# A tower of layers on one core: in the last expert stage half of the tokens go through experts in order of expert

## Chip, core and metric

The kernel runs on one core of a Trainium2 chip. The metric is the device time of one execution in microseconds (us). Before the change it is 6574.02 us, the median of three runs.

## What is computed

The kernel is a stack of embedding, attention and feed-forward layers over 64 x 256 = 16384 tokens of 64 numbers. The change touches only the last feed-forward layer, in which each token goes through the best two of 16 experts:

```python
def _L3_ffn_ref(x, gate_w, gate_b, w1, w2, w3):
    logits = jnp.einsum('bsd,de->bse', x, gate_w) + gate_b
    probs = jax.nn.softmax(logits, axis=-1)
    top_probs, top_idx = jax.lax.top_k(probs, 2)
    top_probs = top_probs / jnp.sum(top_probs, axis=-1, keepdims=True)
    dispatch = jnp.sum(jax.nn.one_hot(top_idx, n_experts, dtype=x.dtype) * top_probs[..., None], axis=-2)
    h1 = jnp.einsum('bsd,edh->bseh', x, w1)
    h2 = jnp.einsum('bsd,edh->bseh', x, w2)
    hidden = jax.nn.silu(h1) * h2
    expert_out = jnp.einsum('bseh,eho->bseo', hidden, w3)
    return jnp.einsum('bseo,bse->bso', expert_out, dispatch)
...
h = h + _L3_ffn_ref(_layernorm(h, axis=-1), ...)
```

## The kernel before

All tokens live in SBUF as 128 tiles of 128 tokens: `H` is the residual stream, `X` a second array of that shape, `XT` the normed tokens turned, two tiles at a time (partitions 0 to 63 hold the numbers of one token, 64 to 127 those of a token of the other tile). Each part of the program is a `Stage`: it takes tiles and semaphores, runs one block of programs for the engines, and ends in a barrier of all engines. So an engine that is late holds the next stage. Inside a stage the order on each engine is the order in the code, and engines meet at semaphores.

The end of the program is four stages. `ln_f3` norms `H` and turns it into `XT`. `routd` (`route`) computes the 16 logits of each token (PE), the softmax and the two best experts (some 30 steps on DVE over 128x2048 numbers, each waiting for the one ahead of it, `link`), and turns the gates into `GT`; meanwhile SP loads the experts' matrices (`tables_d`). `expd` (`experts`) is dense: every token goes through every expert. It is a loop of 256 units, 16 blocks of 1024 tokens by 16 experts. One unit u is

- `hp` and `h`: x times w1 and x times w2 of the expert (L927, four products of 64 rows by 512 columns, the two halves of the array side by side),
- `gp`: the gate spread over 128 rows (L945, bf16),
- ACT: silu of `hp` (L1005); DVE: times `h` (L1041, the product), then times `gp` (L1046, the hidden part),
- `yp`: the hidden part times w3 (L959), added up in PSUM over the 16 experts.

On PE the order is gate(u), out(u-1), first(u+1), second(u+1). `h` and `gp` have one buffer each: second(u+1) waits until DVE has made product u, gate(u+1) until it has made hidden part u. After 16 units the block is turned back (L968) and DVE adds it to `H` (L1028). `store` writes `H` out.

Stages of other layers stand in for operations that `expd` lacks. `expb` gathers, for each of 64 samples, a row of weights per partition by an indirect transfer of POOL into six buffers `chosen` (L2190), multiplies 64x128 weights with 128 columns (L2217, 4 products), then the second matrices (L2230, 4 products), and turns back (L2238). `attd` is attention with f32 products of 128 columns or fewer. L2877 scatters 128 times 128 rows to DRAM, L3440 gathers as many.

## Time and profile before

| what | value |
|---|---|
| median of three runs (6570.31 to 6598.52) | 6574.02 us |
| the profiled execution's own time | 6573.63 us |
| its span | 6570.7 us |
| PE busy, share of the span | 81% |
| DVE, ACT, POOL busy | 78%, 40%, 31% |

The span is what the engines' instructions cover in the profiled execution; 2.9 us lie around it. Shares are means over many stages with different limits, and say nothing of the last stage alone.

### The profile page before, as it was taken

Reading aid. Unit: us, or ns where it says so; the run is one execution under the profiler, and the core shown is the slowest. Engines: PE = TensorE matmul, PEld = TensorE weight load, DVE = VectorE, ACT = ScalarE, POOL = GpSimd, SP = SyncE. Lnnn points to the kernel's source line nnn. Section 1 sums busy time; section 2 is a strip of 40 time slices with the busy share of each in tenths; the row PEclk is TensorE's granted clock in tenths of the full one; section 3 lists DMA queues with packets and bytes.
Section 4 is the critical chain, followed back from the end, with each engine's and each line's share of the span. In section 5 each row is a group of like instructions: output and inputs, shape, how many; then the busy total and the mean of one; then the engine's idle time right before and its main releaser. Section 6 shows DMA issues by size and latency. Waiting matters only on the chain. (4 is left out here: it accounts for less than half of the span.)

```text
span 6570.7 us, 109019 instructions
## 1 busy us (share of the span) xinstructions
PE 5313.6 (81%) x41259; PEld 3459.5 (53%) x41259; DVE 5093.1 (78%) x8887; ACT 2625.4 (40%) x4350; POOL 2046.0 (31%) x1992
## 2 busy tenths in 40 slices
PE   5668968885379999970899999999902899499998
PEld 3552246653246666650788888888801278333332
DVE  7878988886878888850798999989934677677776
ACT  3444433333256666640344444444411422233332
POOL 0010010003267600007777777777743010100000
PEclk8779989996689999975999999999956999699999
DMA  0200000112221000000222222222100000100001
GB/s 17 78 6 1 20 23 29 35 41 73 63 39 18 15 2 2 2 35 13 37 46 41 43 43 41 46 41 45 37 18 4 2 3 3 17 1 1 1 1 26
DMA packets 186692, 165.50 MB, mean 25 GB/s; under 512 B 87754, under 2 KB 167795, under 8 KB 184499
## 3 DMA queue, kind: packets, MB, share of 16 engines
q1 hardware_dynamic: 128814, 126.99, 6.6%
q0 software_dynamic: 57472, 32.64, 4.3%
q8 instruction: 274, 4.49, 0.3%
q14 instruction: 120, 0.98, 0.1%
q10 hardware_dynamic: 12, 0.39, 0.0%
HBM read 87.17 MB, written 50.67 MB: 21 GB/s over the span
## 5 line engine op out<-in xcount | busy, mean ns | idle before, releaser
L3043 PE MATMUL edges_bank<-part_room,hot_room 128*128 128x512 f32 x7168 | 1632.5, 390 | 190.4 <-DVE hot_room L3134 189.4
L3043 PEld LDWEIGHTS edges_bank<-part_room,hot_room 128*128 128x128 f32 x7168 | 1344.4, 188 | 478.6 <-issue 189.8
L3031 POOL DMA_INDIRECT XT<-gat_node_table,edges_idx x1152 | 1206.6, 1047 | 416.2 <-issue 413.2
L3064 ACT COPY XT<-edges_bank 128x512 f32<-128x512 f32 x896 | 524.5, 599 | 946.2 <-PE edges_bank L3043 943.3
L3152 DVE COPY_PREDICATED XT<-edges_tabs_p,XT 128x1024 f32<-128x1024 int32 (+3 forms) x896 | 634.2, 708 | 41.0 <-DVE edges_acc_s L3200 7.3
L3134 DVE TENSOR_SCALAR hot_room<-edges_lanes,edges_nodes 128x512 fp32r<-128x512 f16 x896 | 396.7, 503 | 102.1 <-PE edges_bank L3043 99.1
L1005 ACT ACTIVATE expd_act_out<-expd_hp 128x1024 f32<-128x1024 f32 x256 | 261.9, 1023 | 526.0 <-PE expd_hp L927 526.0
L1041 DVE TENSOR_TENSOR expd_act_out<-expd_act_out,expd_h 128x1024 f32<-128x1024 f32 x256 | 312.6, 1221 | 185.8 <-ACT expd_act_out L1005 185.8
L1460 ACT ACTIVATE GT<-attc_sc,attc_nm 128x256 f32<-128x256 f32 x1024 | 399.6, 480 | 37.0 <-DVE attc_nm L1526 36.9
L1474 ACT ACTIVATE GT<-attc_sct 128x1024 f32<-128x1024 f32 x256 | 262.2, 1024 | 325.0 <-PE attc_sct L1394 324.9
L1525 DVE TENSOR_REDUCE attc_mx<-attc_sc 128x4 f32<-128x1024 f32 x256 | 313.3, 1224 | 86.4 <-PE attc_sc L1383 86.2
L1383 PE MATMUL attc_sc<-XT,attc_tT 64*128 64x256 f32 x2048 | 295.2, 407 | 45.6 <-ACT GT L1460 45.5
L1046 DVE TENSOR_TENSOR expd_hid<-expd_act_out,expd_gp 128x1024 f32<-128x1024 f32 x256 | 312.5, 1221 | 8.8
L1530 DVE TENSOR_REDUCE attc_rs<-GT 128x4 f32<-128x1024 f32 x256 | 310.2, 1212 | 1.2 <-ACT GT L1460 1.2
L505 POOL TENSOR_TENSOR ln_f_xn<-H,ln_f_mean 128x1024 f32<-128x1024 f32 x4 | 11.4, 2846 | 945.5 <-DVE ln_f_shift L542 945.5
L927 PE MATMUL expd_hp<-XT,expd_in_w 64*128 64x512 f32 x1024 | 290.6, 644 | 2.4 <-PEq L82 2.1
L1404 PE MATMUL attc_op<-GT,attc_xB 128*64 128x256 f32 x2048 | 277.5, 391 | 6.8 <-ACT GT L1481 1.9
L959 PE MATMUL expd_yp<-expd_hid,expd_in_w 128*64 128x512 f32 x1024 | 276.2, 618 | 1.6 <-DVE expd_hid L1046 1.6
L1394 PE MATMUL attc_sct<-attc_tT,XT 64*128 64x256 f32 x2048 | 266.4, 377 | 1.6 <-DMA attc_tT<-attc_rT 1.0
L927 PE MATMUL expd_h<-XT,expd_in_wg 64*128 64x512 f32 x1024 | 263.3, 591 | 0.0
L1383 PEld LDWEIGHTS attc_sc<-XT,attc_tT 64*128 64x128 f32 x2048 | 185.1, 190 | 144.5 <-issue 116.5
L1766 ACT ACTIVATE X<-attb_r 128x2048 f32<-128x2048 f32 x64 | 120.1, 1877 | 267.8 <-PE attb_r L1723 267.8
(767 smaller groups left out, 9406.8 us busy)
## 6 DMA issues: line engine op xcount, KB each, us to landing
edges_lanes<-gat_places SPq DMA_DIRECT2D x224, 128.0 KB, 3.1
gat_states<-GT SPq DMA_DIRECT2D x32, 768.0 KB, 4.6
XT<-gat_node_table,edges_idx POOLq DMA_INDIRECT x1152
expert_pairs<-in_L_ffn_W_dram SPq DMA_DIRECT2D x48, 256.0 KB
XT<-XT SPq DMA_DIRECT2D x32, 256.0 KB
XT<-XT SPq DMA_DIRECT2D x64, 128.0 KB
XT<-XT SPq DMA_DIRECT2D x128, 64.0 KB
gat_starts<-nodes_zeros SPq DMA_DIRECT2D x4, 1088.0 KB, 8.0
```

The source lines that it names most:

```text
L927: m = nc.tensor.matmul(bank[:, odd, :], w[half, e, :], g.XT[half, i * U:(i + 1) * U], start=True, stop=True)
L1041: nc.vector.tensor_tensor(act_out[:, u % 2], act_out[:, u % 2], h2[:], ALU.mult).then_inc(product_ready, 1)
L1046: nc.vector.tensor_tensor(hid[:, u % 2], act_out[:, u % 2], gp[:], ALU.mult).then_inc(hid_full, 1)
L1383: m = nc.tensor.matmul(sc[(0, 1, 1, 0)[hp]][:, n, a * S:(a + 1) * S], tT[half, b % NB, hp, a * P:(a + 1) * P], x(b, half), start=True, sto ...
L1460: m = nc.scalar.activation(prob[:, hp % 2, n, a, :], sc[(0, 1, 1, 0)[hp]][:, n, a * S:(a + 1) * S], ACT.Exp, bias=nm[:, b % 2, n, hp, a:a ...
L1525: link(vec.tensor_reduce(best, sc[(0, 1, 1, 0)[hp]][:].rearrange("p n (a s) -> p n a s", s=S), AX.X, ALU.max))
L1530: vec.reduce_sum(rs[:, b % 2, :, hp, :], prob[:, hp % 2], AX.X).then_inc(totaled, 1)
L3031: nc.gpsimd.indirect_dma_start(out=rows[:, k, c, :], out_offset=None, in_=q.t_table, in_offset=bass.IndirectOffsetOnAxis(ap=idx[:, k, c:c ...
L3043: m = nc.tensor.matmul(banks[t % BANKS][:], hot[:, (k * GROUPS + j) % 2, b, t, :], parts[:, p, b].rearrange("p u c -> p (u c)"), start=b = ...
L3064: nc.scalar.copy(fetched[:, (k * GROUPS + j) % 2, t].rearrange("p u c -> p (u c)"), banks[t % BANKS][:]).then_inc(fetched_in, 1)
L3134: m = vec.tensor_scalar(hot[:, (k * GROUPS + j) % 2, b], lanes[:, j], nodes[:, b:b + 1], None, ALU.is_equal)
L3152: vec.copy_predicated(half(0, w), taken(s, w), half(w, 2 * w)).then_inc(halved, 1)
```

## The change

The last layer is cut in two. Token tiles 0 to 63 stay dense, as two calls of `experts` with 4 blocks (64 units) each, `expd` and `expe`. Tiles 64 to 127 are sorted by expert. Each of their tokens has two slots in a DRAM array `sorted_in`, where an expert's slots begin at a multiple of 256; 2 x 8192 slots and at most 15 partly filled tiles make `COUNT` = 79 tiles of 256 slots, whatever the data.

- `ln_f3` keeps the normed tokens in `X` too. `route_sorted` takes the place of `route`: gates for the dense half alone, and for the sorted half the slot of each (token, choice), by two bf16 products with a triangle and with ones, a scan over tiles and experts, and a sum; and the row of weights for each tile and partition. SP clears `sorted_in` (5.2 MB of zeros) and lays out `expert_rows`, 1280 bytes for each expert and partition, behind the loads that it had.
- `expd`: POOL scatters, meanwhile, 64 tiles x 2 choices = 128 indirect transfers of 128 rows of 256 bytes.
- `exps` (`sorted_experts`) is new: 79 tiles. SP loads a tile (64 KB, six buffers), POOL gathers the weights of its expert (160 KB, six buffers), PE turns the tile by a plain product with the identity, multiplies (4 products of 64x128 weights with 128 columns), multiplies with w3 (2 products), turns back by a plain product; DVE and ACT move data between, and SP stores 64 KB to `sorted_out`. It starts when all scatters have landed.
- `expe`: POOL fetches, meanwhile, both rows of each sorted token by 128 indirect transfers; DVE takes them eight token tiles at a time (`collect.add`), after every eighth unit: times the gates, sum of two, plus `H`. The last such group comes behind the last unit.

The core of the diff:

```diff
+    def __init__(self, nc, g, st, W1, W2, W3):
+        self.nc, self.g = nc, g
+        self.sources = W1, W2, W3
+        self.E = E = W1.shape[0]
+        self.COUNT = 2 * SORTED * P // SLOTS_TILE + E - 1
+        self.slot = st.sb("slot", [P, SORTED, 2], I32)
...
+        n = self.COUNT * SLOTS_TILE // P
+        sp.dma_start(self.rows_in.rearrange("(p n) d -> p n d", p=P), bc(self.zeros, 1, n)).then_inc(self.cleared, 16)
+        for half in (slice(0, D), slice(D, P)):
+            sp.dma_start(rows[:, half, 0:P], W1).then_inc(self.built, 16)
+            sp.dma_start(rows[:, half, P:2 * P], W2).then_inc(self.built, 16)
+        sp.dma_start(rows[:, :, 2 * P:], W3).then_inc(self.built, 16)
...
+    def scatter(self, pool):
+        pool.wait_ge(self.cleared, 16)
+        for t in range(SORTED):
+            for c in range(2):
+                self.nc.gpsimd.indirect_dma_start(
+                    out=self.rows_in, out_offset=bass.IndirectOffsetOnAxis(ap=self.slot[:, t, c:c + 1], axis=0),
+                    in_=self.g.X[:, TILES - SORTED + t, :], in_offset=None).then_inc(self.scattered, 16)
+
+    def fetch(self, pool):
+        back = self.g.X[:].rearrange("p (t c) d -> p t c d", c=2)
+        for t in range(SORTED):
+            for c in range(2):
+                self.nc.gpsimd.indirect_dma_start(
+                    out=back[:, t, c, :], out_offset=None, in_=self.rows_out,
+                    in_offset=bass.IndirectOffsetOnAxis(ap=self.slot[:, t, c:c + 1], axis=0)).then_inc(self.fetched[t // 8], 16)
+
+    def add(self, v, link, k, target):
+        vec, t = self.nc.vector, slice(8 * k, 8 * k + 8)
+        y = self.g.X[:].rearrange("p (t c) d -> p t c d", c=2)[:, t]
+        x = target[:, TILES - SORTED + 8 * k:TILES - SORTED + 8 * k + 8, :]
+        v.wait_ge(self.fetched[k], 256)
+        link(vec.tensor_tensor(y, y, bc(self.gate[:, t, :], 3, D), ALU.mult))
+        link(vec.tensor_tensor(y[:, :, 0, :], y[:, :, 0, :], y[:, :, 1, :], ALU.add))
+        link(vec.tensor_tensor(x, x, y[:, :, 0, :], ALU.add))
...
+                link(vec.tensor_tensor(sort.gate[:], sort.gate[:], bc(total[:, DENSE:], 2, 2), ALU.mult))
...
+                link(vec.tensor_copy(tot, pl[:, 1].rearrange("p t e -> p e t")))
+                flat = [a.rearrange("p e t -> p (e t)") for a in (first, keep, tot)]
+                link(vec.tensor_tensor_scan(flat[0], flat[1], flat[2], 0.0, ALU.mult, ALU.add))
...
+                link(vec.tensor_tensor(rank, first.rearrange("p e t -> p t e"), pl[:, 0], ALU.add))
+                link(vec.tensor_tensor(prod, hots, bc(rank, 1, 2), ALU.mult))
+                link(vec.reduce_sum(place, prod, AX.X))
+                link(vec.tensor_copy(sort.slot[:].rearrange("p t c -> p c t"), place))
+                link(vec.tensor_tensor(reach, bc(number[:], 2, E), bc(end[:], 1, COUNT), ALU.is_ge))
+                link(vec.reduce_sum(expert[:], reach, AX.X))
+                link(vec.tensor_scalar(expert[:], expert[:], float(E - 1), float(P), ALU.min, ALU.mult))
+                link(vec.tensor_scalar(sort.weight_row[:], expert[:], g.lane[:], None, ALU.add))
...
+def sorted_experts(nc, g, name, sort):
+
+    COUNT = sort.COUNT
+    NX, NW, NY, NH = 6, 6, 4, 3
+    LAG = NX + 5
...
+                sp.wait_ge(sort.scattered, 16 * 2 * SORTED)
+                for i in range(COUNT + LAG):
+                    if i < COUNT:
+                        if i >= NX:
+                            sp.wait_ge(x_turned, i - NX + 1)
+                        sp.dma_start(xs[:, i % NX], rows_in[i]).then_inc(loaded[i % NX], 16)
+                    k = i - LAG
+                    if k >= 0:
+                        sp.wait_ge(rows_ready, k + 1)
+                        sp.dma_start(rows_out[k], ys[:, k % NY]).then_inc(stored[k % NY], 16)
...
+                for j in range(COUNT):
+                    if j >= NW:
+                        pool.wait_ge(used, j - NW + 1)
+                    nc.gpsimd.indirect_dma_start(
+                        out=chosen[:, j % NW, :], out_offset=None, in_=sort.weights,
+                        in_offset=bass.IndirectOffsetOnAxis(ap=sort.weight_row[:, j:j + 1], axis=0)).then_inc(gathered[j % NW], 16)
...
+                def turn(j):
+                    pe.wait_ge(loaded[j % NX], 16 * (j // NX + 1))
+                    if j:
+                        pe.wait_ge(x_moved, j)
+                    nc.tensor.matmul(pt[:, 0:P], xs[:, j % NX].rearrange("p a d -> p (a d)"), g.ident[:], start=True, stop=True).then_inc(x_turned, 1)
+
+                def hidden(j):
+                    pe.wait_ge(gathered[j % NW], 16 * (j // NW + 1))
+                    pe.wait_ge(x_moved, j + 1)
+                    if j >= 2:
+                        pe.wait_ge(hid_full, j - 1)
+                    for n in range(2):
+                        for a, half in enumerate(halves):
+                            m = nc.tensor.matmul(hp[j % 2][:, a, n * P:(n + 1) * P], chosen[half, j % NW, n * P:(n + 1) * P],
+                                                 xT[half, j % 2, :], start=True, stop=True)
+                    m.then_inc(hp_full, 1)
+
+                def out(j):
+                    pe.wait_ge(hid_full, j + 1)
+                    if j >= 2:
+                        pe.wait_ge(y_moved, j - 1)
+                    for a, half in enumerate(halves):
+                        m = nc.tensor.matmul(yp[j % 2][half, 0:P], chosen[:, j % NW, 2 * P:], hid[:, j % NH, a, :],
+                                             start=True, stop=True)
+                    m.then_inc(used, 1)
+
+                def turn_back(j):
+                    pe.wait_ge(y_moved, j + 1)
+                    if j:
+                        pe.wait_ge(rows_ready, j)
+                    nc.tensor.matmul(yt[:, 0:P], yT[:, j % 2, :], g.ident[:], start=True, stop=True).then_inc(y_turned, 1)
+
+                turn(0)
+                for i in range(COUNT + 3):
+                    if i + 1 < COUNT:
+                        turn(i + 1)
+                    if i < COUNT:
+                        hidden(i)
+                    if 2 <= i < COUNT + 2:
+                        out(i - 2)
+                    if i >= 3:
+                        turn_back(i - 3)
...
+                        nc.scalar.activation(act_out[:, i % 2], hp[i % 2][:, :, 0:P], ACT.Silu).then_inc(act_done, 1)
...
+                def move_x(j):
+                    v.wait_ge(x_turned, j + 1)
+                    if j >= 2:
+                        v.wait_ge(hp_full, j - 1)
+                    vec.tensor_copy(xT[:, j % 2, :], pt[:, 0:P]).then_inc(x_moved, 1)
+
+                def move_rows(j):
+                    v.wait_ge(y_turned, j + 1)
+                    if j >= NY:
+                        v.wait_ge(stored[j % NY], 16 * (j // NY))
+                    vec.tensor_copy(ys[:, j % NY].rearrange("p a d -> p (a d)"), yt[:, 0:P]).then_inc(rows_ready, 1)
+
+                move_x(0)
+                for i in range(COUNT + 4):
+                    if i + 1 < COUNT:
+                        move_x(i + 1)
+                    if i >= 4:
+                        move_rows(i - 4)
+                    if i < COUNT:
+                        v.wait_ge(act_done, i + 1)
+                        if i >= NH:
+                            v.wait_ge(used, i - NH + 1)
+                        vec.tensor_tensor(hid[:, i % NH], act_out[:, i % 2], hp[i % 2][:, :, P:2 * P], ALU.mult).then_inc(hid_full, 1)
...
+def experts(nc, g, name, tables, target=None, hide=0, measure=False, first_block=0, blocks=None, spread=None, collect=None):
 
     E, F, gated = tables.E, tables.F, tables.gated
...
+                    if collect is not None and u and u % COLLECT == 0:
+                        collect.add(v, link, u // COLLECT - 1, target)
...
+                if collect is not None:
+                    for k in range((NU - 1) // COLLECT, SORTED // 8):
+                        collect.add(v, link, k, target)
...
-    turned_norm(nc, g, "ln_f3", g.H, known=True)
+    turned_norm(nc, g, "ln_f3", g.H, keep=g.X, known=True)
     with Stage(nc, "expd_in") as kept:
         tables_d = ExpertTables(nc, kept, I["L3_ffn_w1"], I["L3_ffn_w3"], Wg=I["L3_ffn_w2"])
-        route(nc, g, "routd", I["L3_ffn_gate_w"], I["L3_ffn_gate_b"], 16, probs=True, ahead=tables_d)
-        experts(nc, g, "expd", tables_d, target=g.H)
+        sort = ExpertSort(nc, g, kept, I["L3_ffn_w1"], I["L3_ffn_w2"], I["L3_ffn_w3"])
+        route_sorted(nc, g, "routd", I["L3_ffn_gate_w"], I["L3_ffn_gate_b"], sort, ahead=tables_d)
+        experts(nc, g, "expd", tables_d, target=g.H, blocks=4, spread=sort)
+        sorted_experts(nc, g, "exps", sort)
+        experts(nc, g, "expe", tables_d, target=g.H, first_block=4, blocks=4, collect=sort)
```

What the order on the engines becomes. First PE, where `expd` now ends and the sorted stage begins (`exps_pt` is the turned tile, `exps_hp` the two first products, `exps_yp` the output, `exps_yt` the tile turned back). Before, these rows stood there, with no end:

```order
L927 MATMUL expd_hp<-XT,expd_in_w 128x512 x2
L927 MATMUL expd_h<-XT,expd_in_wg 128x512 x2
L945 MATMUL expd_gp<-GT,expd_in_pick 128x512 x2
L959 MATMUL expd_yp<-expd_hid,expd_in_w 64x512 x2
L927 MATMUL expd_hp<-XT,expd_in_w 128x512 x2
```

And now, after 64 such units:

```order
L1271 MATMUL expd_yp<-expd_hid,expd_in_w 64x512 x4
L1280 MATMUL expd_yt<-ident,expd_yT 128x128 x4
L1216 UNCONDITIONAL_BRANCH
L1098 UNCONDITIONAL_BRANCH
L1104 MATMUL exps_pt<-ident,XT 128x128 x2
L1113 MATMUL exps_hp<-exps_xT,exps_chosen 128x128 x4
L1104 MATMUL exps_pt<-ident,XT 128x128
L1113 MATMUL exps_hp<-exps_xT,exps_chosen 128x128 x4
L1104 MATMUL exps_pt<-ident,XT 128x128
L1113 MATMUL exps_hp<-exps_xT,exps_chosen 128x128 x4
L1122 MATMUL exps_yp<-exps_hid,exps_chosen 64x128 x2
L1130 MATMUL exps_yt<-ident,exps_yT 128x128
```

Per tile PE has eight products of 128 columns, in the order turn of the next tile, first products of this one, output of the one two ahead, turn back of the one three ahead.

POOL had nothing behind the routing stage:

```order
L832 IOTA routd_rev 128x16
L779 MEMSET GT 128x4096
L872 MEMSET expd_in_pick 128x1024
L879 AFFINE_SELECT expd_in_pick<-expd_in_pick 128x2048 x6
L707 UNCONDITIONAL_BRANCH
```

Now it issues 335 indirect transfers, one group in each of the three stages:

```order
L878 DMA sorted_in<-X,expd_in_slot 20224x64 x128
L1216 UNCONDITIONAL_BRANCH
L81 ISA
L1088 UNCONDITIONAL_BRANCH
L1094 DMA exps_chosen<-expert_rows,expd_in_weight_row 128x320 x79
L1072 UNCONDITIONAL_BRANCH
L81 ISA
L1222 UNCONDITIONAL_BRANCH
L886 DMA X<-sorted_out,expd_in_slot 128x64 x128
```

A stage's barrier now waits for POOL to have issued its group.

On DVE the two steps of a unit alternated without a break but for L1028:

```order
L1041 TENSOR_TENSOR expd_act_out<-expd_act_out,expd_h 128x1024
L1046 TENSOR_TENSOR expd_hid<-expd_act_out,expd_gp 128x1024
L1041 TENSOR_TENSOR expd_act_out<-expd_act_out,expd_h 128x1024
L1046 TENSOR_TENSOR expd_hid<-expd_act_out,expd_gp 128x1024
L1041 TENSOR_TENSOR expd_act_out<-expd_act_out,expd_h 128x1024
```

In `expe` three steps of `collect.add` stand between two units, seven times, and once at the end:

```order
L1353 TENSOR_TENSOR expe_act_out<-expe_act_out,expe_h 128x1024
L1358 TENSOR_TENSOR expe_hid<-expe_act_out,expe_gp 128x1024
L895 TENSOR_TENSOR X<-X,expd_in_gate 128x1024
L896 TENSOR_TENSOR X<-X 128x8x64
L897 TENSOR_TENSOR H<-H,X 128x512
L1353 TENSOR_TENSOR expe_act_out<-expe_act_out,expe_h 128x1024
L1358 TENSOR_TENSOR expe_hid<-expe_act_out,expe_gp 128x1024
```

## Rows read from the trace of the kernel before

**Rows 1.** Windows; busy us (count) by engine, granted clock, DMA share, GB/s.

```profile
...
5735.00:5800.00 65.00, 65.00 (x294) 20.41 (x290) 50.14 (x42) 22.06 (x22) 0.00 (x0) 1.00 0.00 1
```

**Rows 2.** Timeline, one steady unit of `expd`; start, length, engine.

```profile
...
6100.85 1.22 DVE L1046 TENSOR_TENSOR expd_hid<-expd_act_out,expd_gp 128x1024 f32<-128x1024 f32 x1
...
6101.47 1.02 PE L927 MATMUL expd_h<-XT,expd_in_wg 64*128 64x512 f32 x4
...
6102.33 0.38 PE L945 MATMUL expd_gp<-GT,expd_in_pick 64*128 64x512 bf16 x2
...
6102.74 1.22 DVE L1041 TENSOR_TENSOR expd_act_out<-expd_act_out,expd_h 128x1024 f32<-128x1024 f32 x1 [0.67 <-ACT expd_act_out L1005]
```

**Rows 3.** Timeline: start and end of `expd`, and the final store.

```profile
...
5721.16 3.76 ACT L804 COPY GT<-routd_gt 128x1024 bf16<-128x1024 bf16 x4 [0.21 <-PE routd_gt L798]
...
5725.80 0.53 PEld L927 LDWEIGHTS expd_hp<-XT,expd_in_w 64*128 64x128 f32 x4 [2.21 <-issue]
...
5733.26 1.08 PE L959 MATMUL expd_yp<-expd_hid,expd_in_w 128*64 128x512 f32 x4
...
6541.85 1.08 PE L959 MATMUL expd_yp<-expd_hid,expd_in_w 128*64 128x512 f32 x4
...
6546.94 0.69 DVE L1028 TENSOR_TENSOR H<-H,expd_yt 128x512 f32<-128x512 f32 x1 [2.51 <-PE expd_yt L968]
6548.77 14.26 SPq L1089 DMA_DIRECT2D out_dram<-H  x4
```

**Rows 4.** Timeline: two whole-width steps at the end of routing on DVE.

```profile
...
5705.02 2.29 DVE L829 TENSOR_TENSOR routd_G<-routd_G,routd_total 128x2048 f32<-128x2048 f32 x1
...
5714.52 1.23 DVE L789 CAST GT<-X 128x2048 bf16<-128x2048 f32 x1
```

**Rows 5.** Groups of POOL: issuing indirect scatters of 128 rows each.

```profile
...
L2877 POOL DMA_INDIRECT gat_starts<-gat_a_dst,gat_start_row x128 | 124.1, 969 | 82.3 <-issue 41.4 <-DVE gat_a_dst L2860 40.9
```

**Rows 6.** Timeline: the per-sample stage `expb` at the high clock.

```profile
...
1691.34 0.72 PE L2217 MATMUL expb_hp<-XT,expb_chosen 64*128 64x128 f32 x8
...
1691.98 0.66 PE L2230 MATMUL expb_yp<-expb_hid,expb_chosen 128*64 128x128 f32 x8
...
1692.49 1.30 POOL L2190 DMA_INDIRECT expb_chosen<-expert_pairs,expb_idx  x1 [0.30 <-issue]
...
1692.57 0.33 PE L2238 MATMUL expb_yt<-ident,expb_yT 128*128 128x128 f32 x1
...
1692.83 0.71 PE L2217 MATMUL expb_hp<-XT,expb_chosen 64*128 64x128 f32 x8
```

**Rows 7.** Timeline: plain f32 products with 128x128 weights in `attd`.

```profile
...
5457.05 0.59 PE L1940 MATMUL attd_r<-attd_both,XT 128*128 128x192 f32 x2
...
5457.57 0.33 PE L1949 MATMUL attd_r<-attd_vz,attd_kd 128*32 128x32 f32 x16
...
5457.83 0.66 PE L1955 MATMUL attd_r<-attd_wp,attd_oT 128*128 128x64 f32 x4
...
5458.42 1.08 PE L1977 MATMUL attd_r<-X,attd_vz 128*32 128x128 f32 x32
```

**Rows 8.** Groups of DVE: the 128x128 copy out of PSUM.

```profile
...
L2068 DVE COPY attd_vz<-attd_r 128x128 f32<-128x128 f32 x37 | 10.4, 280 | 0.0
```

**Rows 9.** DMA issues: KB each, median us to landing.

```profile
...
edges_lanes<-gat_places SPq DMA_DIRECT2D x224, 128.0 KB, 3.1
```

**Rows 10.** Timeline: `expb` at a granted clock of 0.50.

```profile
...
1575.79 0.48 PE L2238 MATMUL expb_yt<-ident,expb_yT 128*128 128x128 f32 x1
...
1578.40 0.48 PE L2238 MATMUL expb_yt<-ident,expb_yT 128*128 128x128 f32 x1
```

**Rows 11.** Windows, columns as in rows 1: `expb` twice, then the start of `expd`.

```profile
...
1600.00:1650.00 50.00, 29.35 (x225) 20.62 (x225) 21.88 (x42) 15.17 (x40) 14.86 (x13) 0.60 0.55 144
1660.00:1700.00 40.00, 37.56 (x423) 26.69 (x422) 37.70 (x93) 27.25 (x75) 30.30 (x23) 1.00 0.42 119
5725.00:5733.00 8.00, 6.85 (x20) 2.40 (x20) 2.44 (x2) 3.14 (x3) 0.00 (x0) 0.58 0.00 1
```

More of the change, by code:

```diff
@@ L687, in top2_steps, with route @@
     return vector_part, pool_part, act_part
-def route(nc, g, name, Wr, br, E, ahead, probs=False):
+def route(nc, g, name, Wr, br, E, ahead):
     with Stage(nc, name) as st:
@@ L758, in _, with __init__ @@
             def _(act):
-                if probs:
-                    act.wait_ge(shifted, 1)
-                    nc.scalar.activation(L, L, ACT.Exp).then_inc(exped, 1)
-                else:
-                    parts["act"](act)
+                parts["act"](act)
                 gates.scalar(act)
+SORTED, SLOTS_TILE, COLLECT = TILES // 2, 2 * P, 8
 class GateSplit:
-    def __init__(self, nc, g, st, E, scratch):
-        self.nc, self.g, self.E = nc, g, E
-        self.g3 = g.GT[:, TOKENS // 2:].rearrange("p (t c) -> p t c", c=D)
-        self.rest = scratch
+    def __init__(self, nc, g, st, E, scratch, tiles=TILES):
+        self.nc, self.g, self.E, self.tiles = nc, g, E, tiles
+        self.g3 = g.GT[:, TOKENS // 2:].rearrange("p (t c) -> p t c", c=D)[:, 0:tiles]
+        self.rest = scratch[:, 0:tiles]
         self.pt = [st.ps(f"gt{k}", [P, 8 * P], BF16) for k in range(2)]
@@ L792, in tensor @@
         pe.wait_ge(self.split, 1)
-        for c in range(TILES // 16):
+        for c in range(self.tiles // 16):
             if c >= 2:
@@ L801, in scalar @@
     def scalar(self, act):
[L802 removed]
+        for c in range(self.tiles // 16):
             act.wait_ge(self.turned, c + 1)
             self.nc.scalar.copy(self.g.GT[:, c * 8 * P:(c + 1) * 8 * P], self.pt[c % 2][:]).then_inc(self.moved, 1)
[L807 to L835 removed]
 class ExpertTables:
@@ L882, in gpsimd, with sync, clear @@
                 pool.wait_ge(self.picked, done)
-def experts(nc, g, name, tables, target=None, hide=0, measure=False):
+class ExpertSort:
+    def __init__(self, nc, g, st, W1, W2, W3):
[4 more added lines that the diff above has]
+        self.slot = st.sb("slot", [P, SORTED, 2], I32)
+        self.gate = st.sb("gate", [P, SORTED, 2])
+        self.weight_row = st.sb("weight_row", [P, self.COUNT], I32)
+        self.zeros = g.stats[:].rearrange("p t s -> p (t s)")[:, 0:D]
+        self.rows_in = nc.dram_tensor("sorted_in", [self.COUNT * SLOTS_TILE, D], F32).ap()
+        self.rows_out = nc.dram_tensor("sorted_out", [self.COUNT * SLOTS_TILE, D], F32).ap()
+        self.weights = nc.dram_tensor("expert_rows", [E * P, 5 * D], F32).ap()
+        self.built, self.blank, self.cleared, self.scattered, self.own = (
+            st.sem(n) for n in ("rows_built", "blank", "rows_cleared", "scattered", "sort_own"))
+        self.fetched = [st.sem(f"fetched{k}") for k in range(SORTED // 8)]
+    def sync(self, sp):
+        W1, W2, W3 = self.sources
+        rows = self.weights.rearrange("(e p) f -> e p f", e=self.E)
+        sp.wait_ge(self.blank, 1)
+        n = self.COUNT * SLOTS_TILE // P
[4 more added lines that the diff above has]
+        sp.dma_start(rows[:, :, 2 * P:], W3).then_inc(self.built, 16)
+    def clear(self):
+        self.nc.gpsimd.memset(self.zeros, 0.0).then_inc(self.blank, 1)
+    def scatter(self, pool):
[20 more added lines that the diff above has]
+        link(vec.tensor_tensor(x, x, y[:, :, 0, :], ALU.add))
@@ L887, in experts @@
+def experts(nc, g, name, tables, target=None, hide=0, measure=False, first_block=0, blocks=None, spread=None, collect=None):
     E, F, gated = tables.E, tables.F, tables.gated
     U = 512
-    NB = TOKENS // (2 * U)
+    NB = TOKENS // (2 * U) if blocks is None else blocks
     NU = NB * E
@@ L915, in _ @@
                     g.order.sync(sp)
+            @block.gpsimd
+            def _(pool):
+                if spread is not None:
+                    spread.scatter(pool)
+                if collect is not None:
+                    collect.fetch(pool)
             @block.tensor
@@ L926, in hidden @@
                     for odd, half in enumerate(halves):
-                        m = nc.tensor.matmul(bank[:, odd, :], w[half, e, :], g.XT[half, i * U:(i + 1) * U], start=True, stop=True)
+                        m = nc.tensor.matmul(bank[:, odd, :], w[half, e, :], g.XT[half, (first_block + i) * U:(first_block + i + 1) * U], start=True, stop=True)
                     return m
@@ L944, in gate @@
                     for odd, half in enumerate(halves):
-                        m = nc.tensor.matmul(gp[:, odd, :], pick[half, e, :], g.GT[half, i * U:(i + 1) * U], start=True, stop=True)
+                        m = nc.tensor.matmul(gp[:, odd, :], pick[half, e, :], g.GT[half, (first_block + i) * U:(first_block + i + 1) * U], start=True, stop=True)
                     m.then_inc(gp_full, 1)
@@ L1053, in _ @@
                 add(NB - 1)
+                if collect is not None:
+                    for k in range((NU - 1) // COLLECT, SORTED // 8):
+                        collect.add(v, link, k, target)
                 if measure:
```

219 lines of the change are left out of this document (177 added, 42 removed).

## Prediction

> **What bounds the kernel now.** I read the page for the whole, then windows over the last stage, then its timeline. In `expd` PE is busy in 100 us of 100, at a granted clock of 1.00, with DVE at 78 and ACT at 33 [rows 1]. In the timeline DVE is what sits idle: it waits 0.67 us in each unit for ACT [rows 2], which by the code waits for `hp` of PE. So PE is the bound, and the stage costs PE's time per unit. The first `yp` of the stage starts at 5733.26 and the one of unit 254 at 6541.85, so a unit takes (6541.85 - 5733.26) / 254 = 3.183 us, turns back included. The stage runs from 5725.80 to 6546.94 + 0.69 = 6547.63: 821.8 us, of which 256 x 3.183 = 814.9, and 7.0 are filling and emptying [rows 3].
>
> **Removed, and what stays dense.** Two dense stages of 64 units take the place of one of 256: each 64 x 3.183 + 7.0 = 210.7, together 421.4 us.
>
> **The sorted stage, per tile.** PE has eight f32 products of 128 columns. Six of them stand in `expb`, with the same shapes and operands of the same kind. There the four first products take 1691.98 - 1691.34 = 0.64 us from start to start, at the high clock; the four second ones 1692.57 - 1691.98 = 0.59, so the two that are left here some 0.30 [rows 6]. A turn is a plain product with 128x128 weights, which no row has at 128 columns. `attd` brackets it: one of 192 columns takes 5457.57 - 5457.05 = 0.52 us, and two of 64 columns take 5458.42 - 5457.83 = 0.59, 0.295 each [rows 7]. The line between them gives 0.41 for 128 columns. The turn of `expb`, which is in transpose mode, takes 0.26 [rows 6]; that is the lower bound, 0.52 the upper. I take 0.41, twice. A tile: 0.41 + 0.64 + 0.30 + 0.41 = 1.76 us; with the bounds 1.46 to 1.98.
>
> What could be slower than PE? DVE has two copies of 128x128 at 0.28 [rows 8] and a product of 256 columns, below the 0.69 of 512 [rows 3]: at most 1.25 us. ACT has silu over 256 columns and a copy of 128, no more than DVE's work. POOL issues one gather per tile; undisturbed one takes 0.97 us [rows 5] and 0.30 between two [rows 6], 1.27 in all; beside DVE's adds in `expb` 1.30 + 0.30 = 1.60 [rows 6]. All lie below 1.76. The waits in a circle: a tile buffer of weights is reused six tiles on, and the gather may be issued once the output of tile j-6 is made, four tiles ahead of its use: 4 x 1.76 = 7.0 us for 1.27 of issue and the landing. A load of 128 KB lands in 3.1 us [rows 9], so this holds if landing stays under 5.7. Bytes: 160 KB of weights, 64 in and 64 out per tile, 295 KB in 1.76 us = 168 GB/s. `expb` moves 119 GB/s at a DMA share of 0.42 [rows 11], in proportion 0.59 here, and more for the shorter packets. It fits, not with much room.
>
> 79 tiles x 1.76 = 139.0. Before the first turn come a barrier and a load (3.1), behind the last tile three more steps of the pipeline and a store (3.1): about 10 together. The stage begins behind idle time, as `expd` did before, and I let it start at the low clock (1.2 GHz of 2.4) as well: in the first 8 us of `expd` the granted clock is 0.58 [rows 11]. A cycle of `expb` takes 2.61 us at the low clock (1578.40 - 1575.79) [rows 10] and 1.49 at the high one (1692.83 - 1691.34) [rows 6], a factor of 1.75; 8 us at the low clock lose 3.4. The sorted stage: 139.0 + 10 + 3.4 = 152 us.
>
> **The scatters in `expd`.** 128 scatters took (124.1 + 41.4) / 128 = 1.29 us each [rows 5]. So POOL is done after 165 us of the stage's 210.7 and lies wholly beside PE; it would show only above 1.65 us each. The 1.60 of `expb` [rows 6] makes 205, still covered. Rows here are 256 bytes, 16384 of them; the final store moves as many runs of 256 bytes from 6548.77 to the end of the span at 6570.7, in 22 us [rows 3], so bandwidth isn't the question. The zeros (20224 runs of 256 bytes, by the same rate 27 us) and the weights' rows stand on SP behind loads that were there, in a routing stage of 100 us; the scatters wait for the zeros alone. I cost them at nothing; uncovered they would cost at most 40.
>
> *A page on it:* the Trainium skill, "GPSIMD Engine Reference", section "Key points", says that GpSimd shares its SBUF interfaces with VectorE and contends with instructions that have two SBUF inputs. The trace agrees: POOL's issue took 1.30 us beside adds of two SBUF tiles against 0.97 undisturbed. The two steps of an `expd` unit read one SBUF tile and one in PSUM, so by the page the 1.29 holds there; without the page's distinction 1.60 would hold, and the sum is the same.
>
> **The fetches and adds in `expe`.** 16 gathers must land for each eight units: 16 x 1.29 = 20.7 us against 8 x 3.183 = 25.5. Covered. The adds are new work of DVE: 1024, 512 and 512 columns; at 0.69 for 512 [rows 3] that is 1.2 + 0.7 + 0.7 = 2.6 us in one piece. The next product waits anyway 0.67 us for ACT. Behind it PE has little slack: hidden part u ends at 6102.07 and the gate product that waits for it starts at 6102.33, 0.26 [rows 2]. So each piece stops PE for 2.6 - 0.67 - 0.26 = 1.7 us; seven of them, 12, and the eighth stands uncovered behind the last unit, 2.6: 14.5 us. Bounds: 2.6 alone if all is made up, 8 x 2.6 = 21 if nothing is.
>
> **Routing.** A step over 128x2048 takes 2.29 us [rows 4]. Four steps on gates and five of the split shrink to half: 4 x 1.15, and 2 x 1.15 + 3 x 0.62 of the split with its casts (1.23), -9 us. Added behind them are six steps of 1024 numbers, two of 2048, two of 1264, a scan of 1024 and a dozen small ones: 6 x 1.15 + 2 x 2.3 + 2 x 1.4 + 1.2 to 2.4 + 2 = 18 us. But the old stage went on for 9 us after DVE's last cast (5714.52 + 1.23) until the gates were copied (5724.92) [rows 3, 4], and DVE's new steps lie beside that. Net 0 to +1; I take +1, bounds -1 to +4.
>
> **Barriers.** From the last copy of `routd` (5721.16 + 3.76) to the first weights of `expd` (5725.80) pass 0.9 us [rows 3]; two more: 1.8.
>
> **Sum.** 421.4 + 152 + 14.5 + 1 + 1.8 = 590.7 against 821.8: -231.1. The profiled span becomes 6570.7 - 231.1 = 6339.6, with the 2.9 around it 6342.5. The profiled execution (6573.63) and the median (6574.02) differ by 0.4: predicted 6343. The bounds of the terms (1.46 to 1.98 a tile: -24 to +17; adds -12 to +6; routing -2 to +3) give 6305 to 6369.
>
> **Rivals.**
>
> *A, data for the tiles comes late.* Between 1600 and 1650 `expb` issued 13 gathers, 3.85 us a sample, with PE busy 59% and the DMA share at 0.55 [rows 11]: weights can be late, there beside other transfers of SP. For it: three streams at once, and only four tiles of lead. Against it: between 1660 and 1700 the same loop ran at its PE bound. A landing of 8 us makes (8 + 1.27) / 4 = 2.3 us a tile, 79 x 0.55 = +43: 6386. Chance 0.18.
>
> *B, the clock stays low in the sorted stage.* `expb` stayed at 0.50 with PE's products in close order [rows 10], and had 0.60 between 1600 and 1650 [rows 11]. Then a tile takes 1.76 x 1.75 = 3.08 us: 79 x 1.32 - 3.4 = +101: 6444. For it: short products with waits between. Against it: `expb` also kept 1.00 at 94% busy [rows 11]. The Trainium skill, "TensorE: Matmul & The Clock Gate", section "PE-mode transpose", says that transposes don't count as busy for the clock; the turns here are plain products, which would make B less likely, and no row here shows that by itself. Chance 0.12.
>
> *C, indirect transfers of 256-byte rows are slower to issue than the rows shown.* At 2.0 us each, 128 make 256 us, both dense stages grow by 45: 6433. For it: no row has 256 bytes. Against it: in `expb`, whose rows are 1536 bytes, the issue took 1.30 beside adds, and in the scatters, whose rows are 16 bytes, 0.97 [rows 5, 6]; a hundredfold length moved it less than the threshold of 1.65. The Trainium skill, "DMA: Bandwidth & Descriptors", section "Specifications", puts the shortest transfer at full rate at 512 bytes and calls shorter ones read-modify-write; by it the landing suffers, while the issue, which is the term here, does not. Chance 0.07.
>
> *D, slower than before.* A, far worse: the sorted stage eats the gain when a tile takes (139 + 231) / 79 = 4.68 us, which is a landing of 17 us. The worst stretch of `expb`, 3.85, gives 6343 + 79 x 2.09 = 6508; at 5.0 us a tile it would be 6599. Chance 0.03.
>
> That the change doesn't do what it says is hardly possible: 79 tiles and 128 units are fixed, whatever the data.
>
> **How the numbers follow.** The forecast has 0.60, with 6305 to 6369. A 0.18, B 0.12, C 0.07, D 0.03. The range 6300 to 6440 holds the forecast, A, C and milder forms of B, and leaves out most of B and D. A measurement of this kernel tells about 0.5% (33 us) from no change: faster 0.96, within it 0.01, slower 0.03.
>
> **What the profile after would show.** Two dense stages of some 211 and 225 us with PE at 100%; between them a stage of 152 with 79 gathers 1.76 us apart, PE near 100% and the clock 1.00 after its start; POOL done with its scatters 45 us ahead of the barrier; DVE pieces of 2.6 us each with a PE gap of 1.7. Wrong it would be by first products that wait for `exps_chosen` (A, D), a clock near 0.5 between the dense stages (B), or POOL as the last at a barrier or `collect.add` waiting for its rows (C).

## The result, and the profile after

The changed kernel takes 6337.5 us, the median of 4 runs (6328.9 to 6341.7); the kernel before, in 4 runs, 6572.2. The ratio is 0.9634, with a 95% interval of 0.9605 to 0.9663. The forecast was 6343, in a range of 6300 to 6440. The profiled execution took 6341.45 us with a span of 6339.7, 231.0 us under the span of before.

Windows of the changed kernel, with the columns of [rows 1]: `expd`, the start of the sorted stage `exps`, its steady part, and `expe`.

```profile
5736.00:5946.00 210.00, 206.62 (x912) 65.14 (x912) 158.50 (x132) 69.18 (x69) 122.74 (x128) 0.99 0.06 21
5949.00:5965.00 16.00, 15.53 (x83) 11.20 (x84) 4.62 (x15) 3.15 (x10) 7.56 (x8) 0.50 0.51 144
5971.00:6083.00 112.00, 112.00 (x1086) 84.03 (x1087) 61.47 (x204) 43.05 (x136) 62.83 (x67) 1.00 0.67 177
6093.00:6313.00 220.00, 208.06 (x912) 64.09 (x908) 175.70 (x152) 67.89 (x68) 122.81 (x128) 0.99 0.10 20
```

PE is the bound of all three stages; in `expe` it stands idle for 12 us of 220, which are the adds below. In the steady part of `exps` it is busy in 112 us of 112 at a clock of 1.00. The second line is the surprise: 16 us at 0.50 (1.2 GHz), with PE busy in 15.5 of them.

The timeline of PE in the steady part shows what a tile costs:

```profile
6042.67 0.44 PE L1122 MATMUL exps_yp<-exps_hid,exps_chosen 128*64 128x128 f32 x4
6043.04 0.49 PE L1130 MATMUL exps_yt<-ident,exps_yT 128*128 128x128 f32 x2
6043.36 0.39 PE L1104 MATMUL exps_pt<-ident,XT 128*128 128x128 f32 x2
6043.68 0.71 PE L1113 MATMUL exps_hp<-exps_xT,exps_chosen 64*128 64x128 f32 x8
6044.32 0.44 PE L1122 MATMUL exps_yp<-exps_hid,exps_chosen 128*64 128x128 f32 x4
```

From start to start: outputs 0.37, the turns 0.32 each, first products 0.64; the tile 6044.32 - 6042.67 = 1.65 us.

The boundary between routing and `expd`, from the timeline of the changed kernel, where the old one had [rows 3, 4]:

```profile
5714.68 0.69 DVE L776 CAST GT<-XT 128x1024 bf16<-128x1024 f32 x1
...
5718.21 2.29 DVE L1007 TENSOR_TENSOR_SCAN XT<-XT 128x1024 f32<-128x1024 f32 x1
...
5718.64 1.93 ACT L791 COPY GT<-routd_gt 128x1024 bf16<-128x1024 bf16 x2 [0.21 <-PE routd_gt L785]
...
5734.60 0.26 DVE L1025 TENSOR_SCALAR expd_in_weight_row<-routd_expert,lane 128x79 int32<-128x79 f32 x1
5736.02 2.08 PE L1239 MATMUL expd_hp<-XT,expd_in_w 64*128 64x512 f32 x4 [16.50 <-PEq L82]
```

The gates are copied at 5720.57, and DVE goes on alone for 14 us; PE waits 16.5 us at the barrier.

An add piece in `expe`, from the timeline of the changed kernel:

```profile
6123.30 1.22 DVE L895 TENSOR_TENSOR X<-X,expd_in_gate 128x1024 f32<-128x1024 f32 x1
...
6124.55 0.69 DVE L896 TENSOR_TENSOR X<-X 128x512 f32<-128x512 f32 x1
6124.96 1.13 PE L1239 MATMUL expe_hp<-XT,expd_in_w 64*128 64x512 f32 x4
6125.28 0.69 DVE L897 TENSOR_TENSOR H<-H,X 128x512 f32<-128x512 f32 x1
...
6127.28 1.13 PE L1239 MATMUL expe_h<-XT,expd_in_wg 64*128 64x512 f32 x4 [1.19 <-DVE expe_act_out L1353]
...
6129.86 1.13 PE L1239 MATMUL expe_hp<-XT,expd_in_w 64*128 64x512 f32 x4
```

`hp` to `hp` takes 4.90 us here, 3.15 in an undisturbed unit: the piece costs 1.75 us.

The groups of POOL; the last columns are busy time, mean, and idle time:

```profile
L886 POOL DMA_INDIRECT X<-sorted_out,expd_in_slot x128 | 123.0, 961 | 50.7 <-issue 38.7 <-SPq L1216 12.0
L878 POOL DMA_INDIRECT sorted_in<-X,expd_in_slot x128 | 122.7, 959 | 128.7 <-SPq L1216 87.3 <-issue 41.4
```

(122.7 + 41.4) / 128 = 1.28 us for a scatter.

**The span, term by term.** The first normalising step of `ln_f` on DVE (the reciprocal) started at 5600.42 before and starts at 5605.78 now: 5.4 us of drift in stages that nothing touches. From there to `expd`'s first weights it was 125.4 us and is 130.2: +4.8 for routing. Then, from the first weights of `expd` to the last add of `expe`, 580.5 us (`expd` 210.3, `exps` with its barriers 146.1, `expe` 224.1) against 821.8: -241.3. What comes behind is 0.1 longer. The sum is 5.4 + 4.8 - 241.3 + 0.1 = -231.0.

### The profile page after: what moved, and what is told of

It is laid out like the page before. It is cut to its first block and busy times, and to the rows that moved or that the text cites. A ratio compares the mean times of both kernels' runs of the same rounds, so it can differ in the third digit from the quotient of the medians.

```text
span 6339.7 us, 108731 instructions
## 1 busy us (share of the span) xinstructions
PE 5054.9 (80%) x40671; PEld 3433.3 (54%) x40671; DVE 4882.0 (77%) x8912; ACT 2538.3 (40%) x4368; POOL 2373.4 (37%) x2332
## 5 line engine op out<-in xcount | busy, mean ns | idle before, releaser
L1711 PEld LDWEIGHTS attc_sct<-attc_tT,XT 64*128 64x128 f32 x2048 | 204.7, 188 | 21.1 <-DMA attc_tT<-attc_rT 1.9
L2379 DVE TENSOR_TENSOR X<-attd_r,attd_decay 128x2048 f32<-128x2048 f32 x64 | 146.7, 2291 | 82.2 <-PE attd_r L2282 82.1
L1721 PEld LDWEIGHTS attc_op<-GT,attc_xB 128*64 128x64 f32 x2048 | 129.4, 136 | 128.0 <-issue 94.0
L2127 DVE TENSOR_REDUCE attb_mx<-attb_r 128x16 f32<-128x2048 f32 x64 | 146.4, 2287 | 65.7 <-PE attb_r L2026 65.6
```

What stands on the lines that cost most here:

```text
L1711: m = nc.tensor.matmul(sct[:, n, j * S:(j + 1) * S], x(b, half)[:, j * P:(j + 1) * P], tT[half, b % NB, hp, :], start=True, stop=True)
L1721: m = nc.tensor.matmul(op[half, 0:S], xB[:, b % NB, j, (2 * hp + n) * D:(2 * hp + n + 1) * D], probT[:, hp % 2, n, j, :], start=hp + j == ...
```

## The experiments

A run's whole time drifts: the same kernel reached routing's first product at 5635.1, 5641.9 and 5626.2 us in three executions. So I compare the lengths of four stretches: routing (first `logits` product to first `hp`), `expd` (to the end of its last add), `exps` (to the first `hp` of `expe`), `expe` (to the first store). The code of the edits is abridged.

```
kernel         chip  routing   expd    exps    expe
changed          -    101.0    210.2   146.1   225.8
e0_again         A    101.0    210.1   146.4   225.8
e1_transpose     A    101.0    210.1   161.3   225.7
e2_direct        A    100.9    210.1   222.8   226.6
e3_spread        A    101.0    210.1   146.4   213.0
e4_later         B     92.5    366.3   144.7   377.3
e5_warm          B    101.0    362.6   146.1   377.0
e6_lead          B    101.0    363.4   189.7   378.0
e7_twice         B    101.0    527.2   146.9   376.8
e9_best          C     92.5    214.1   146.5   212.9
e10_wide         C    101.0    210.3   132.0   225.9
e11_twice        C    101.0    210.1   264.2   226.6
e12_again        C    101.0    210.1   148.8   225.7
```

Three chips were used, each in one batch of runs. On A the kernel before took 6573.5 us, on C 6569.3, on B 7877.9. Of the runs in the table only the changed kernel and e9 were executed more than once, four times each.

**e0_again.** 

> The changed kernel once more, unaltered, to see how far the lengths of single stages repeat: expd 210.3, exps 146.1, expe 224.2 us, each within 0.5 us; the stages ahead may differ by some us in sum.

The stages repeat within 0.3 us. Over all runs that leave the sorted loop alone `exps` repeats less well: 144.7 us (e4) to 148.8 (e12), without e5. What differs is how long the granted clock stays at 0.50 behind the first turn: 14 us in e4, 17 in the changed kernel, 23 in e12. So a difference of some 2 us in `exps` says nothing.

**e1_transpose.**

```
-  nc.tensor.matmul(pt[:, 0:P], xs[...], g.ident[:], start=True, stop=True)
+  nc.tensor.transpose(pt[:, 0:P], xs[...], g.ident[:])
   (the turn back likewise)
```

> Both turns of the sorted stage in PE's transpose mode in place of plain products with the identity; nothing else. In the profile after, the two turns together take 0.64 us and a tile 1.655 us. (a) A turn costs what the one of expb costs, 0.26 us: a tile 1.53 us, the stage 9 us shorter than its 146.1. (b) Both forms cost the same: stage unchanged, 146. (c) Turns in transpose mode keep the clock low for longer than the first 16.5 us: each tile at the low clock costs 1.3 us more; low throughout it would be 214 us and more. I expect (a).

Measured: 161.3 us, 15 longer. Windows of e1_transpose over `exps`:

```profile
5950.00:6000.00 50.00, 50.00 (x295) 31.50 (x293) 18.89 (x63) 13.65 (x42) 19.80 (x22) 0.50 0.47 126
6000.00:6020.00 20.00, 20.00 (x190) 13.43 (x190) 11.15 (x41) 8.29 (x26) 12.43 (x14) 0.91 0.66 181
6020.00:6040.00 20.00, 17.70 (x180) 11.58 (x177) 10.76 (x40) 8.26 (x26) 12.69 (x14) 1.00 0.73 203
6040.00:6080.00 40.00, 40.00 (x248) 25.45 (x248) 15.37 (x51) 11.04 (x34) 15.82 (x17) 0.53 0.48 128
```

It is (c), with (a) inside it: where the clock is 1.00 a tile is shorter than with plain products, but the clock is 0.50 for the first 58 us and falls again later. PE in the timeline of e1_transpose at the clock of 1.00:

```profile
6028.53 0.33 PE L1130 MATMUL exps_yt<-ident,exps_yT 128*128 128x128 f32 x1
6028.70 0.27 PE L1104 MATMUL exps_pt<-ident,XT 128*128 128x128 f32 x1
6028.90 0.71 PE L1113 MATMUL exps_hp<-exps_xT,exps_chosen 64*128 64x128 f32 x8
6029.54 0.44 PE L1122 MATMUL exps_yp<-exps_hid,exps_chosen 128*64 128x128 f32 x4
6029.91 0.33 PE L1130 MATMUL exps_yt<-ident,exps_yT 128*128 128x128 f32 x1
```

The two turns take 6028.90 - 6028.53 = 0.37 us in place of 0.64, and a tile 6029.91 - 6028.53 = 1.38 us, where (a) had 1.53. At 0.50 a tile takes 2.40. By the Trainium skill, "TensorE: Matmul & The Clock Gate", section "PE-mode transpose", transposes don't count as busy for the clock; this trace agrees, with PE busy in 50 us of 50 at 0.50. It does not single the transposes out, since the next run has such a stretch without any.

**e2_direct and e10_wide.** In both the second products come out as rows, with no turn back:

```
-  matmul(yp[half, 0:P], chosen[:, 2*P:], hid[:, a, :])      # then ACT copy, turn_back, DVE copy
+  matmul(yp[:, a*D:(a+1)*D], hid[:, a, :], chosen[:, 2*P:])   # e2: 64 columns, ACT copies to ys
+  matmul(yp[:, a*P:(a+1)*P], hid[:, a, :], chosen[:, 3*D:])   # e10: 128 columns, half not used
```

> The second products of the sorted stage with the hidden values as weights and the expert's matrix as 64 columns, so that rows come out with slots on partitions: the turn back, ACT's copy for it and DVE's second copy are gone. (a) Such a product costs what those of 64 columns in attd cost, 0.295 us: 0.59 for the two in place of 0.37 + 0.32, a tile 1.56 us, and one step of the pipeline less behind the last tile: the stage 9 us shorter than 146.1. (b) With only 64 columns to hide it, the load of 128x128 weights sets the pace and the product costs 0.4 us: a tile 1.77, the stage 8 us longer. (c) PE is not what bounds the stage: no change. I expect (a).

> As e2_direct (hidden values as weights), but with 128 columns moved in each second product instead of 64; the additional 64 columns (a part of another matrix) are made and not used. In e2_direct the granted clock was 0.50 in the whole sorted stage, 2.73 us a tile with PE busy all the time. (a) It was the 64-column products that kept the clock low: with 128 columns it comes back to 1.00, a tile takes 0.32 + 0.64 + 0.64 = 1.60 us, the stage about 143 us. (b) It was the exchange of weights and moved operand, or the missing turn: the clock stays at 0.50, a tile takes over 2.8 us, the stage 225 us or more. I expect (a).

Measured: e2 222.8 us, e10 132.0. Windows of e2_direct, then of e10_wide:

```profile
5965.00:6020.00 55.00, 55.00 (x283) 45.95 (x282) 14.64 (x41) 13.10 (x40) 18.89 (x20) 0.50 0.41 109
6020.00:6170.00 150.00, 150.00 (x771) 125.39 (x770) 39.12 (x110) 35.67 (x110) 51.02 (x54) 0.50 0.39 107
```

```profile
5974.00:6050.00 76.00, 75.86 (x708) 63.73 (x706) 35.83 (x101) 32.40 (x100) 47.53 (x51) 1.00 0.70 197
```

And PE in the timeline of e10_wide:

```profile
6030.30 0.71 PE L1121 MATMUL exps_yp<-exps_chosen,exps_hid 128*128 128x128 f32 x4
6030.84 0.39 PE L1103 MATMUL exps_pt<-ident,XT 128*128 128x128 f32 x2
6031.16 0.72 PE L1112 MATMUL exps_hp<-exps_xT,exps_chosen 64*128 64x128 f32 x8
6031.81 0.71 PE L1121 MATMUL exps_yp<-exps_chosen,exps_hid 128*128 128x128 f32 x4
```

None of e2's three cases foresaw it. PE was busy in 205 us of 205 (5965 to 6170), as my case (a) has it, but at 0.50 to the end of the stage, where its tile of 2.73 us makes the stage 77 us longer. e10 has the same order of products and moves 128 columns in the second ones: the clock is 1.00 from 12 us behind the last add of `expd` on, the two products take 0.54 us, a tile 1.51 (1.60 expected), and the stage is 14 us shorter than that of the changed kernel, 17 shorter than e12's on the same chip. So the exchange of weights and moved operand, (b), is not what kept e2 at 0.50, since e10 has it too; case (a) of e10 holds. Nor is it the share of weight loads: PEld is busy in 84% of the stretch in both (125.39 of 150, 63.73 of 76). e2 ran on chip A and e10 on chip C; the unaltered kernel came to a clock of 1.00 on both, so the chip is an unlikely cause.

**e3_spread.**

```
-  if u and u % COLLECT == 0: collect.add(v, link, u // COLLECT - 1, target)
+  if u >= 7 and u % 7 < 3 and u // 7 <= SORTED // 8:
+      collect.add(v, link, u // 7 - 1, target, u % 7)      # one of the three steps
-  for k in range((NU - 1) // COLLECT, SORTED // 8): collect.add(...)   # behind the last unit
```

> The adds of expe in 24 single steps instead of 8 pieces of three: one step behind the DVE work of each of units 7, 8, 9, then 14, 15, 16 and so on, the last at 58, none behind the last unit. (a) A step stalls PE only by what exceeds 0.93 us (DVE's wait for ACT and PE's slack): 0.3 for the gate step of 1.22 us, nothing for the two of 0.69: expe falls from 224.2 us to 210.7 + 2.4 = 213. (b) Every step of DVE stalls PE by its whole length: 8 x 2.6 = 21 us, expe 231. (c) The stall comes from waiting for the fetched rows, not from DVE's time: expe longer than 224, with DVE waiting for DMA. I expect (a).

Measured: `expe` 213.0, 12.8 us shorter. (a) holds: the units behind which a gate step stands are 0.15 to 0.35 us longer, 2.4 in all, and no other step shows. The burst cost the time, not DVE's work.

**e9_best, with e4_later in it.** e4 issues the steps from L1019 on in `expd`:

```
+  if spread is not None and u < len(spread.later): step = spread.later[u](); link(step)
+  pool.wait_ge(self.placed, 1)            # in scatter(), before the first one
```

> DVE's last seven steps of routing (slots and weight rows, 5726.45 to 5734.86 in the profile after, 8.4 us) are issued in expd instead, one behind the DVE work of each of the first seven units; the scatters wait for the third. (a) The routing stage gets 8.4 us shorter, and expd loses only what exceeds 0.93 us in each step: 1.4 + 1.4 + 0.6 + 0.6 = 4.0 us; net -4.4 from the end of the norm to the start of the sorted stage. (b) DVE's time comes back whole: net 0. (c) The scatters start some 12 us later and become the last at the barrier: not by the rows, they were done 46 us ahead. I expect (a).

> The adds of expe in single steps (as in e3_spread, which took 12.8 us from expe) together with the deferred routing steps (as in e4_later, which took 8.4 us from routing). Expected on a chip where scatters do not disturb PE: routing 92.5, expd 210.3 + 4.0 = 214.3, exps 146.1, expe 212.9: 17 us under the changed kernel, 0.3%, and about 0.961 of the kernel before. If DVE's deferred time comes back whole, expd is 218.7 and the gain is that of the adds alone, 13 us.

e4 ran on chip B, where `expd` can't be compared (below); its routing is 8.5 us shorter. e9, on chip C, has the same 92.5 and an `expd` of 214.1, +4.0 against e12 on the same chip, where 4.0 was expected. e9 took 6315.8 us (4 runs), 0.9611 of the kernel before (0.9595 to 0.9627), and 19.4 us less than e12_again on the same chip; 2.3 of these lie in `exps`, where e12 was late to the high clock, so the two edits are worth the 17 us forecast. The interval overlaps with that of the changed kernel's ratio; it is the stages that show the gain. e10's edit lies in another stage. By an estimate from e10's `exps`, 132.0 in place of 146.5, both together would come to some 6301; that was not run.

**e12_again.** 

> The changed kernel unaltered, as the measure for the other three: routing 100.9, expd 210.3, exps 146.1, expe 225.7 us to the store. On a chip where the scatters hold up PE: expd near 363, expe near 377, and then more time than the kernel before.

`exps` is 2.4 us longer than in e0: two more tiles ran at a granted clock of 0.50, at 2.93 us in place of 1.66. The others repeat.

**e5_warm.**

```
+  for _ in range(3): nc.tensor.matmul(pt[:], g.ident[:], g.XT[:, 0:512], start=True, stop=True)
   turn(0)
```

> Three f32 products of 512 columns whose result is not used stand ahead of the first turn of the sorted stage, in the 3.4 us in which PE waits for the first load. (a) The low clock of the stage's first 16.5 us (granted 0.50) comes from that idle stretch: filled, the low stretch is short or gone, and the stage some 7 us shorter than 146.1. (b) The clock has fallen for the barrier's idle time already, or the short products of the fill do not bring it back: the low stretch stays at some 16 us and the stage within 1 us. The granted clock between the barrier and the tenth tile tells. I expect (a), with little confidence.

Measured: 146.1, no change that shows beside the 144.7 and 146.9 of e4 and e7 on the same chip. (b) is right on the stage's length; on the clock neither case is right. Windows of e5_warm from the start of the stage:

```profile
7394.00:7398.00 4.00, 2.50 (x4) 1.26 (x5) 0.69 (x1) 0.00 (x0) 1.56 (x2) 0.76 0.22 57
7398.00:7402.00 4.00, 3.52 (x17) 1.86 (x15) 0.58 (x2) 0.14 (x1) 3.08 (x4) 0.82 0.66 192
7402.00:7406.00 4.00, 2.45 (x25) 1.71 (x25) 1.58 (x5) 1.06 (x4) 1.66 (x3) 1.00 0.54 155
7406.00:7410.00 4.00, 4.00 (x24) 3.10 (x26) 1.28 (x5) 0.65 (x2) 1.33 (x2) 0.54 0.21 65
7410.00:7414.00 4.00, 4.00 (x29) 2.89 (x26) 1.13 (x4) 1.28 (x4) 0.98 (x2) 0.61 0.49 129
```

The granted clock fell to 0.50 at 7396.1, 2.1 us behind the last dense product and in the first of the three, rose to 1.00 at 7399.5, and was 0.50 again from 7406.3 to 7413.1, behind a stretch in which PE, in the filling pipeline, was busy 2.45 us of 4. It is back at 1.00 for good 18.4 us behind the last add, 19.4 in the changed kernel. The fillers also held the first turn back: 5.1 us behind the last add instead of 2.7. That the one gain and the other loss cancel is argued from these numbers, not tested.

**e6_lead.** `NW` is 4 in place of 6.

> Four buffers for gathered weights instead of six. A buffer is busy for wait and issue (1.25 us), landing (3.1), then from the first product to the output two tiles on, 2T + 1.0 us. (a) If the weights' way round the buffers bounds, 4T = 5.35 + 2T gives T = 2.7 us a tile, the stage 146 + 79 x 1.0 = 227 us; with six buffers the same sum gives 1.34, below PE's 1.655, which is why data was not late there. (b) If landing is short when the queue is less loaded, T stays near 1.66 and the stage at 146. I expect (a).

Measured: 189.7 us, (189.7 - 146.1) / 79 = 0.55 more a tile: 2.2 us, with 38.0 us of PE's waits for `exps_chosen`. (a) in kind, half its size; solved backwards, 4T = x + 2T + 1.0 gives x = 3.4 us for issue and landing, not 5.35 - 1.0 = 4.35. With six buffers weights would be late from x = 5.6 on.

**e7_twice and e11_twice.** The same edit, on chips B and C:

```
-  for c in range(2):
-      indirect_dma_start(out=self.rows_in, ...)
+  for c, rows in ((0, self.rows_in), (1, self.rows_in), (0, self.again), (1, self.again)):
+      indirect_dma_start(out=rows, ...)
```

> Each scatter of expd is issued twice, the second time into a scratch array that nobody reads: 256 instead of 128. (a) POOL's issue at 1.28 us each becomes the bound of the stage: 256 x 1.28 = 328 us instead of 210.3, expd +117. (b) The transfers themselves, not the issue, are what takes the time, and they were hidden in the issue's shadow: more than 1.28 each and SP's wait for landed rows some us behind POOL's last issue. I expect (a), and PE at 100% for the first 210 us.

> e7_twice once more: each scatter issued twice, the second into a scratch array that nobody reads. On the chip of the first four experiments: (a) POOL's issue bounds the stage, 256 x 1.28 = 328 us, PE done with its 64 units after 210 us, expd +118; (b) scatters hold up PE, as on the other chip, where one unit took 39.2 us beside them: then expd is near 527 us.

e11 ran on chip C, not on that of the first four experiments, A. There (a) holds: PE is done after 210.1 us, and the end of the stage behind it, which waits for the scatters, comes 118 us later (264.2 - 146.1), as 256 x 1.28 - 210 says. A little of (b) is in it: POOL's last issue ends at 6060.2 and SP's first load starts at 6063.5, so the wait for landing is 3.3 us; the granted clock is back at 1.00 9 us behind the first turn there, not 17, and that gives them back. On chip B `expd` took 527 us, and 363 with the 128 scatters of the changed kernel. ACT in the timeline of e7_twice, and windows of e5_warm beside the scatters and behind them:

```profile
7241.02 1.02 ACT L1318 ACTIVATE expd_act_out<-expd_hp 128x1024 f32<-128x1024 f32 x1 [38.18 <-remote]
7280.22 1.02 ACT L1318 ACTIVATE expd_act_out<-expd_hp 128x1024 f32<-128x1024 f32 x1 [38.18 <-remote]
```

```profile
7061.00:7190.00 129.00, 23.85 (x50) 5.24 (x50) 8.55 (x7) 3.25 (x4) 95.85 (x101) 0.50 0.07 25
7215.00:7390.00 175.00, 175.00 (x776) 54.76 (x772) 134.64 (x112) 57.07 (x57) 0.00 (x0) 0.99 0.00 1
```

POOL issues at its usual 1.27 us, but PE is busy in 24 us of 129, and one unit takes 39.2 us (7280.22 - 7241.02), against 3.15 elsewhere. When POOL stops, PE is back at 100%. The DMA share is 0.07, so the DMA engines are not full. What holds the engines up is open: ACT and DVE start long after what they wait for, and the profile calls the releaser "remote".

It is not every gather. On the same chip `exps`, with 79 gathers, took the usual 146.1 us, and `expb`, with 64, 166.1 in e5 against 167.6 in e12. In both POOL waits for PE between gathers. Where it mostly issues one behind another the time grew, in unaltered stages too: `edges` with its 1152 gathers took 2736 us in e5 against 1660 in e12, `attc` beside 256 of them 1268 against 1044. These 1300 us are about what separates the kernel before on B from that on C. Whether it is the issue without pauses or the shorter rows (256 bytes in `expd`, 1280 in `exps`) was not tested. All four runs on chip B are of one batch, so the chip and the moment are not told apart. There the changed kernel with e5's three products took 7941.2 us, 0.8% more than the kernel before, each executed once.

## Why the prediction was right

- **Dense stages:** 2 x 210.7 forecast. 210.3 and, without the adds' share, 224.1 - 12.2 - 2.7 = 209.2; `expe` starts behind a shorter pause, and its first unit takes 3.5 us against 4.5 in `expd`.
- **Tile:** 1.76 forecast, 1.65 measured. The turn, a line between two widths of `attd` [rows 7], was set at 0.41 and takes 0.32; the outputs, half of `expb`'s second products [rows 6], at 0.30 and take 0.37. Over 79 tiles that is -8.3 us, the largest miss.
- **Low clock at the start:** 3.4 forecast from the first 8 us of `expd` [rows 11]. It held for 17 us behind the first turn: six tiles took 14.9 us (first `hp` at 5950.93, seventh at 5965.86) instead of 9.9, 5.0 lost, and somewhat more since the first tiles lack outputs and turns back.
- **Scatters and fetches hidden:** right. The last scatter is issued 46 us ahead of the end of `expd`; e11 shows that what POOL needs beyond the dense stage's 210 us comes out whole.
- **Adds:** 1.7 a piece forecast, 1.75 measured; 14.5 in all, 12.2 + 2.7 = 14.9 measured. e3 confirms the working, slack included.
- **Routing:** the one term outside its own bounds. +1 forecast with +4 as bound; +4.8 measured. From the first search for the best expert to the end of the split the old routing took 44.9 us and the new takes 39.2, so 5.6 were saved, not 9. The nine steps counted did shrink and gave back 8.1. What I had not counted took 2.5: one more step for `both` (1.1), three steps cut into two halves of 1.23 (0.2 each), and three small ones (0.7). What comes behind took 19.3 us, not 18.
- **Sum:** tile -8.3, routing +3.8, low clock +1.6, the rest -2.4, drift upstream +5.4. They cancel. The mechanism was the one forecast, with PE as the bound of all three stages; the hit within 0.1 us of the span is luck, since the misses happen to cancel, 5.4 us of drift in stages that the change doesn't touch among them. The median is 5.5 us below the forecast.
- **Rivals:** A did not occur (in the steady part PE never waits for `exps_chosen`), though e6 shows how near it is, and at 1.38 us a tile (e1) PE did wait for `exps_chosen` now and then. B did not occur with the form of products chosen; e1 and e2 bring it about by that form alone. C did not occur: 1.28 us, not 2.0, and no more than 1.30 on any chip. D, as a long tile, did not occur, but on chip B the kernel is slower than before by a way I had not listed: scatters that hold up the other engines. I had weighed POOL's issue against PE's time, and never asked whether other engines run at full speed beside it.

## What to carry to other kernels

A loop of short products is to be costed at both clocks, and the granted clock read again after each change of their form: here transposes or 64-column products in place of plain 128-column ones cost more than they saved, and of two loops that differ in 64 columns that nobody uses, the one that moves them was 91 us shorter. Work of DVE beside a PE-bound loop is free as long as each single step fits into the slack of one unit, so spread it step by step. Work hidden beside a long unbroken issue of indirect transfers by POOL should be measured on more than one chip.
